# A gated block of recurrence and feed-forward layer on one core: three small groups of adding transfers, a transfer of token factors placed earlier in SyncE's list, a loop over chunks written out, and weight units of the first chunk placed earlier

## The reference

```python
def wkv(time_decay, time_first, k, v):        # along T, per channel
    w, u = -jnp.exp(time_decay), time_first
    def step(carry, kv_t):
        aa, bb, pp = carry
        kt, vt = kv_t
        q = jnp.maximum(pp, u + kt)
        e1, e2 = jnp.exp(pp - q), jnp.exp(u + kt - q)
        y_t = (e1 * aa + e2 * vt) / (e1 * bb + e2)
        q2 = jnp.maximum(pp + w, kt)
        e1b, e2b = jnp.exp(pp + w - q2), jnp.exp(kt - q2)
        return (e1b * aa + e2b * vt, e1b * bb + e2b, q2), y_t
    ...

def ffn(x, W1, W2, W3):
    hidden = jax.nn.silu(x @ W1.T) * (x @ W3.T)
    return fwht(hidden) @ W2.T

x = x + jnp.tanh(g_xattn[0]) * wkv(time_decay, time_first, layernorm(x), ctx)
x = x + jnp.tanh(g_ffn[0]) * ffn(layernorm(x), W1, W2, W3)
```

## Time and profile before

| | |
|---|---|
| three runs | median 1058.67 us (1058.36 to 1063.57) |
| profiled execution | 1061.08 us, span 1059.3 us |
| PE, DVE, ACT, POOL busy | 1002.8, 805.1, 440.5, 239.9 us |
| mean share of the 16 DMA engines in use | 0.94 from 100 to 150 us, 0.49 from 400 to 500 us |

### The profile page before, as it was taken

How to read it: one execution, slowest core, us unless ns; L and a number is a source line. 1 busy time by engine, 2 the same in 40 slices (tenths; PEclk the granted TensorE clock), 3 DMA queues, 4 the chain that set the end, 5 groups by cost and what they waited for, 6 DMA issues and landing times.

```text
span 1059.3 us, 18211 instructions
## 1 busy us (share of the span) xinstructions
PE 1002.8 (95%) x6892; PEld 684.3 (65%) x6892; DVE 805.1 (76%) x1316; ACT 440.5 (42%) x736; POOL 239.9 (23%) x180
## 2 busy tenths in 40 slices
PE   5799998769999999999999999999999999999998
PEld 2365443346677777777776677776777777767775
DVE  7857998869989995889667995889669994653334
ACT  5766451336244443455243443455243542422221
POOL 0130121101432133221421033321422124211111
PEclk9899999889999999999999999999999999999999
DMA  9977999994885446354644356354745434444331
GB/s 357 319 284 267 286 263 307 216 328 168 292 290 188 153 187 239 120 200 152 265 160 180 127 193 238 105 201 161 268 163 178 155 126 159 160 159 156 131 153 40
DMA packets 47398, 214.27 MB, mean 202 GB/s; under 512 B 9200, under 2 KB 24688, under 8 KB 36208
## 3 DMA queue, kind: packets, MB, share of 16 engines
q1 hardware_dynamic: 40816, 200.52, 51.7%
q0 software_dynamic: 6496, 12.58, 5.7%
HBM read 183.70 MB, written 41.97 MB: 213 GB/s over the span
## 4 chain that ended last, share of the span: by engine, by line
PE 66%; DVE 13%; DMA 12%; issue 6%; ACT 2%; SPq 1%; POOL 0%; DVEq 0%; ACTq 0%
PE pl L743 8%; PE pl L741 8%; PE pl L742 8%; PE po L753 7%; PE po L755 7%; PE pg L741 6%; PE pg L742 6%; PE pg L743 6%; DMA up_sums<-w_t 5%; DMA up_sums<-up_sums 4%; PE po L764 4%; PE po L762 4%; DVE x L1435 1%; DVE work L1628 1%; DVE eb L1284 1%
## 5 line engine op out<-in xcount | busy, mean ns | idle before, releaser
L1756 POOL TENSOR_TENSOR work<-work 128x512 bf16<-128x512 f32 x112 | 164.2, 1466 | 604.6 <-DVE work L1628 604.6
L753 PE MATMUL po<-work,w 128*128 128x512 f16 x456 | 173.0, 379 | 1.7 <-DVE x L1435 0.7
L755 PE MATMUL po<-work,w 128*128 128x512 f16 x456 | 172.8, 379 | 0.0
L1071 ACT ACTIVATE work<-work 128x256 f32<-128x256 f32 x168 | 68.0, 415 | 210.1 <-DVE work L1535 209.9
L741 PE MATMUL pg<-wts 128*128 128x256 f16 x448 | 122.5, 273 | 13.5 <-DVE work L1535 13.4
L1535 DVE TENSOR_TENSOR work<-pl,wts 128x256 f32<-128x256 f32 x168 | 65.2, 415 | 81.5 <-PE pl L743 79.9
L741 PE MATMUL pl<-xn,wts 128*128 128x256 f16 x448 | 122.4, 273 | 0.0
L743 PE MATMUL pg<-wts 128*128 128x256 f16 x448 | 122.4, 273 | 0.0
L742 PE MATMUL pl<-wts 128*128 128x256 bf16 x448 | 122.4, 273 | 0.0
L741 PE MATMUL pl<-wts 128*128 128x256 f16 x448 | 122.4, 273 | 0.0
L743 PE MATMUL pl<-wts 128*128 128x256 f16 x448 | 122.4, 273 | 0.0
(11 more groups left out here) (207 smaller groups left out, 2138.3 us busy)
## 6 DMA issues: line engine op xcount, KB each, us to landing
wts<-up_stage SPq DMA_DIRECT2D x56, 2048.0 KB, 7.9
up_stage<-wts SPq DMA_DIRECT2D x8, 1024.0 KB, 10.2
up_stage<-wts SPq DMA_DIRECT2D x16, 512.0 KB, 7.9
ev<-ctx_t SPq DMA_DIRECT2D x7, 1024.0 KB, 10.3
xin<-x_t SPq DMA_DIRECT2D x7, 1024.0 KB, 7.6
bv<-x_tok SPq DMA_DIRECT2D x7, 1024.0 KB, 9.6
out_t<-x SPq DMA_DIRECT2D x7, 1024.0 KB, 4.5
wts<-w_t SPq DMA_DIRECT2D x4, 1024.0 KB, 11.6
```

The costliest lines, as they stand in the source:

```text
L753: pe.matmul(po[:, d, :], w2h[:, j, d * P:d * P + P], hh[:, b, :], start=start, stop=False, skip_group_check=True)
L755: pe.matmul(po[:, d, :], w2l[:, j, d * P:d * P + P], hh[:, b, :], start=False, stop=False, skip_group_check=True)
L1071: act.activation(sg[:, slot, cols], src, ACT.Silu, scale=(1.0, -1.0)[slot]).then_inc(acted, 1)
L1756: pool.tensor_tensor(hl[:, b, :], hf[:, slot, :], hh[:, b, :], ALU.subtract).then_inc(pair_lo, 1)
```

## The change

There are five edits.

- `GROUPS` becomes three groups of two pieces each.
- In SP's list, `put_sums(6)` and `spread_factors(Run(3))` now stand ahead of `load_again(8)`, and `load_tokens(1)` ahead of `load_unit(10)`.
- The loop over runs 3 to 6 is written out (`middle_runs`), with constant counts.
- `unit_hi(4)` and `unit_lo(4)` move from slot 0 of run 1 to beside slot 3 of run 0; `unit_hi(5)` stands ahead of the work on the second weights in slot 0; units 5 to 11 move a slot or less ahead (`unit_slot`).
- The moments of run 3's tokens (`next_tok`) move from slot 12 to slot 11.

```diff
 FIRST_AT = dict(tok=2, tok_norm=3, exps=((4, 0), (4, 2), (5, 0), (5, 2)), weigh=6, scan_b=6, den=7, log=7, scan_a=7,
                 num=8, inv=8, over=9, resid=9, mean=(11, 1), centre=10, square=11,
-                sum_var=11, var=(13, 0), rsqrt=13, norm=14, next_tok=12)
+                sum_var=11, var=(13, 0), rsqrt=13, norm=14, next_tok=11)
...
-GROUPS = ((2, 4), (4, 8))
+GROUPS = ((2, 4), (4, 6), (6, 8))
...
-        def run_loop(eng, body):
-
-            with eng.Fori(0, 2) as i:
-                body(Run(i * 2 + 3, 0, i + 1))
-                body(Run(i * 2 + 4, 1, i + 1))
+        def middle_runs(body):
+
+            for r in range(3, 7):
+                body(Run(r, 1 - r % 2, (r - 1) // 2))
...
-        unit_slot = {0: (4,), 1: (5, 6), 2: (7, 8), 3: (9,), 4: (10, 11), 5: (12,), 9: (13,), 10: (14,), 11: (15,)}
+        unit_slot = {0: (5, 6), 1: (7, 8), 2: (9,), 3: (10,), 4: (11,), 5: (12,), 9: (13,), 10: (14,), 11: (15,)}
...
             load_x(1)
-            load_unit(10)
             sp.wait_ge(xn_turned, 4)
             load_tokens(1)
+            load_unit(10)
             load_unit(11)
...
             put_factors(Run(3))
+            put_sums(6)
+            spread_factors(Run(3))
             load_again(8)
-            spread_factors(Run(3))
-            put_sums(6)
             load_again(9)
...
-            run_loop(sp, steady)
+            middle_runs(steady)
...
                     if j == 0:
+                        unit_hi(5)
                         for i in range(11, 14):
                             tile_hi(i)
...
                     for n in unit_slot.get(j, ()):
-                        unit_hi(n)
+                        if n > 5:
+                            unit_hi(n)
...
             turned_hi(1)
+            unit_hi(4)
             silu(a, 3)
...
             hidden_tile(a, 3)
+            unit_lo(4)
             ffn(b)
```

More of the change, by code:

```diff
@@ L861, in _ @@
             pairs(Run(2, 1, 0))
-            run_loop(pe, pairs)
+            middle_runs(pairs)
             pairs(Run(7, 0, 3))
@@ L1166, in _ @@
             pairs(Run(2, 1, 0))
-            run_loop(act, pairs)
+            middle_runs(pairs)
             pairs(Run(7, 0, 3))
@@ L1670, in _ @@
             hidden_tile(a, 3)
+            unit_lo(4)
             ffn(b)
             pairs(Run(2, 1, 0))
-            run_loop(dve, pairs)
+            middle_runs(pairs)
             pairs(Run(7, 0, 3), more=False)
@@ L1778, in _ @@
             pairs(Run(2, 1, 0))
-            run_loop(pool, pairs)
+            middle_runs(pairs)
             pairs(Run(7, 0, 3))
```

## The result

The changed kernel takes 1056.82 us (median of 12 runs, 1054.86 to 1059.82), the kernel before beside it on the same chip 1061.01 us. The ratio is 0.9967, with an interval of 0.9953 to 0.9981: a gain of 0.33%, some 4 us, where 13.3 us were predicted. The time lies above the predicted range.

The account below looks back on a forecast made before the run. The prediction took DVE's list to bound the kernel up to about 285 us and PE's after it. Gains of 8.8 + 1.0 + 3.5 = 13.3 us from 1058.67 gave 1045.4 us, range 1039.5 to 1051.5.

Parts of the forecast that it names:

- Part 1: Weight units and run 2's tokens, slots 0 to 5: DVE takes slot 5's tile sooner, 1.5 us (bounds 0.7 and 1.7).
- Part 2: Moments in slot 11 cover slot 12's 4.18 us stop, less 0.7 us waiting for tokens: 3.5 us (bounds 2 and 4.2).
- Part 3: Spread of run 3's factors ahead of the scaling: it starts at 210.0 instead of 218.83, 8.8 us including both earlier parts.
- the factors land near 202.9: Ahead of the scaling: the factors land behind run 2's big load, no sooner than before, and the spread lands at 209.9.
- rival B: Thicker DMA crowd in 140 to 200 us; tokens, sums' buffer or factors come later: 7.0 us gained, 1051.7 us; chance 0.23.
- The ring order: Run 3's factors share a ring with run 2's 2 MB load, consumed in order, so they cannot pass it.
- the 4.2 forecast: Ahead of the scaling, 4.2 us of DVE's 8.01 us wait stay: it starts at 210.0 and not at 205.8.
- Part 4: Clock in pair 0: PE waits less, so half of DVE's 2.06 us stop goes, 1.0 us (bounds 0 and 2.1).
- The prediction's own formula: PE's wait in pair 0: 8.31 us, plus 5.0, minus the 8.8 gained up to the scaling, gives 4.5 us.
- Part 5: Loop over runs 3 to 6: without the jump back its stop goes, 3.5 us (below 3.0, or 4.1 with the loop's ends).
- C: Front edits do nothing, another transfer releases the scaling at the old time; only the loop's 3.5 us: 1055.2 us; chance 0.07.
- D: The third group of adding transfers is late and holds later loads and PE: 33 us slower, 1092 us; chance 0.03.

Follow-up runs that it names:

- e2: The changed kernel with the adding transfers in the two groups of before, all other edits kept: 1053.72 us, ratio 0.9923.
- e15: The kernel before with the three groups of adding transfers and nothing else: 1060.31 us, ratio 0.9987.
- e5: The changed kernel without the adding transfers, so the weights of units 4 to 15 are wrong: 1046.29 us, ratio 0.9844.
- e7: The changed kernel with run 3's factors written as 128 pieces instead of 1024 and read back in a wrong order: 1044.75 us, ratio 0.985.
- e10: The changed kernel, three groups, with every run's factors written in 128 pieces and read back correctly with a stride: 1065.12 us, ratio 1.0036.
- e13: The changed kernel, three groups, with the factors of run 3 alone in 128 pieces, read back with a stride: 1049.76 us, ratio 0.9877.
- e14: The changed kernel with two groups and the factors of run 3 alone in 128 pieces, read back with a stride: 1048.05 us, ratio 0.9873.
- e3: The changed kernel with run 3's factors put ahead of put_sums(5) and of run 2's first load in SP's list: 1055.71 us, ratio 0.9932.
- e4: The changed kernel with run 3's factors issued by ScalarE in slot 13 instead of by SP: one run, 1050.27 us, the kernel before 1060.90 beside it.
- e6: The changed kernel measured again, unchanged: 1055.91 us, ratio 0.9944.
- e8: The changed kernel with the third group's adding transfers held until the factors have landed: 1060.02 us, ratio 0.9979.
- e1: The kernel before with only its loop over runs 3 to 6 written out: 1059.74 us, ratio 0.9983.
- e9: The changed kernel with two groups and run 3's tokens, moments, factors and spread moved sooner: 1053.6 us, ratio 0.9936.

## Why the prediction was wrong

**Part 1 was right.** It said 1.5 us. DVE took slot 5's tile at 110.57, 37.49 us from the mark; before it was 109.57 - 70.52 = 39.05. That is 1.6 us. The stop of 3.39 us stayed, and PE's product was what DVE waited for, as put.

**Part 2 was right in its sum, 3.5 us, in part by luck.** Both parts made DVE free for the scaling 5.0 us sooner, exactly the sum. In detail it differed: the tokens were there without a wait, and a new stop of 1.61 us for the next sums' buffer stood behind them. With these edits but two groups (e2) DVE waited 1.56 us for the tokens and was free 3.6 us sooner, of which Part 2 has 2.0, its lower bound. e15 shows, besides, that the three groups alone take 2.4 us off the stop of 4.18: the edits cover the same wait, and their gains don't add.

**Part 3 failed,** at the step "the factors land near 202.9", that is, at their flight of 14 us. From the mark, the scaling began at 145.3 us where it had been 148.3: 3.0 us gained and not 8.8. The flight was taken as 14 us because "they stood behind" the big load. Without the adding transfers it is 14.5 us (e5), with 128 pieces 13 to 15 (e7, e10, e13, e14): for the floor the figure was good. On SP's queue they did run behind the load: in the changed kernel 21 and 13 packets under 512 bytes are recorded in 191 to 194 and 194 to 197 us, while that queue moved 1.21 and 1.07 MB, and 295 in the next 3 us. But that was not what made the flight long: put ahead of the load (e3), or on another queue (e4), they took 26.5 and 27.1 us. What the step left out is the turn-taking with the packets of the other queues (e4), here those of the adding transfers, which makes it 18.3 us in two groups (e2) and 22 to 23 in three (the changed kernel, e6). Without those adds (e5, and e8, where only the third group was held: 13.9 us) or with few small packets (e7) it is gone. From the mark the factors were issued 2.6 us sooner than before (115.7 against 118.3) and landed at 138.6, where 132.4 had been put. The third group's adds begin at 188.05 and 190.67 us, with the factors issued at 188.79. So the edit of the groups worked against that of the spread, inside one change; the mechanism belongs to rival B, but the working had no price for it.

I had the rows for a doubt: the earlier trace rows show 443 packets of 512 to 2048 bytes beside 560 small ones, and I read only the small ones. (They ran 8 to 14 us behind their issue, not 9 to 14.) I also took the window in which the small packets were recorded for the landing, where e5 has 6.7 us between the two.

The Trainium skill, page DMA: Bandwidth & Descriptors, section Queues, rings and completion order, says that a DMA engine takes turns between the rings it has work for, a packet at a time. The equal counts on the three queues of e4 agree, and the 368 beside 339 here; in the other two windows shown above they are 295 beside 320 and 302 beside 197. The ring order that I cited from the same section agrees with the packets on SP's queue, but it did not decide the landing.

**With two groups the prediction's steps come nearer.** From the mark, e2's scaling began at 213.27 - 72.19 = 141.1, 7.2 us sooner than before (8.8 put). Its stop of 4.35 us is near the 4.2 forecast because two terms were off alike: DVE was free 1.4 us later than put, and the factors landed 2.1 us later. In all e2 gained 9.7 us from the mark, 8.5 between the medians, of the 13.3.

**Part 4 failed with Part 3.** It said 1.0 us. PE after, in pair 0, against the earlier trace rows:

```profile
225.94 0.40 PE L740 MATMUL pg<-wts 128*128 128x256 f16 x1 [7.60 <-DVE work L1537]
```

That is 7.60 us where 4.5 were put; the clock fell as before and DVE's stop stayed at 2.06 us. The prediction's own formula would give 8.31 + 5.0 - 3.0 = 10.3 us for this wait, so it was off as well. Where the stop ahead of the scaling was halved (e2), DVE's stop was 0.98 us, as the term has it, but behind a wait of PE of 2.99 us; with 2.64 us (e4) there was no such stop, and with 1.96 us (e14) it was 1.16. Taking half of 2.06 was a guess that e2 happened to meet.

**Part 5 had the right mechanism, and a term was missing.** The stop at the jump back is gone, 3.5 us. But the other intervals are longer by 0.34 us in the mean, so 1.8 us stay (e1, and 593.58 - 591.80 here). I had seen that the runs outside the loop were 0.3 us longer and counted this as a possible gain; it was the price.

**The sum by what ran:** 3.0 ahead of the scaling, 0 for the clock, 1.8 for the loop: 4.8 us from the prediction's terms, 4.3 measured from the mark, 4.2 between the medians. Of the rivals, B is nearest in kind but gave 7.0 (its 1051.7 us lies just outside the range that was to reach over most of it). C gave 1055.2 with another mechanism (another transfer releases the scaling at the old time). D did not happen.

**Still open:** why turns cost as much as they do. 1024 packets of 4 bytes pass in 3 us without adds, and take three or four such windows beside them. In the trace of the kernel before, the adding packets take about 0.16 us each where they are alone (140 packets, 45.6% of 16 engines in 206 to 209 us), and in e3, with as many small packets beside them, 0.36 us (156 packets, 117.4% in 194 to 197). They are slow in themselves, then, and slower in company; what a packet waits for is not shown. Nor is it shown what makes a written-out run longer.

## What to carry to other kernels

When a small scattered transfer gates a step, look at what else is in flight in its window, by count of packets and not by bytes, and ask of every other edit whether it puts more there. A transfer's landing is read from what it releases, not from when its packets are recorded. Fewer pieces cure it, but if an engine then reads with a stride, the price is paid at every read: pack only the transfer that gates, and leave the steady part as it is.

## What the runs showed of the hardware

- A write of 1024 elements of 4 bytes took 14.5 us to report without adding transfers beside it, 18.3 with them in two groups (at most 15.9 when issued sooner, e9), 21.8 and 22.9 in three, and 26.5 and 27.1 in three when put ahead of the load (e3) or on ScalarE's queue (e4). 128 pieces of 32 bytes took 12.8 to 14.8 us beside the same adds.
- Three queues with work had equal numbers of packets in 3 us, whatever their size: 119, 117 and 117 (e4).
- VectorE's product or sum of 128x1024 elements takes 0.81 us more (1.61 to 2.42, and 1.21 to 2.02 us) when one f32 operand is read at a step of 32 bytes, with its access cut in two dimensions. The Trainium skill, page SBUF — State Buffer, section Door 1: The DMA port swizzle, says that reads which cross to a new line of 16 bytes each time pay a penalty; the rows agree.
- A run written out takes 118.2 to 118.6 us, one inside the loop 117.9, one that enters or leaves the loop 118.2, and the jump back cost 3.5 us once.
- The time from a fixed row early in the program repeated to 0.3 us between two executions of the changed kernel (984.5 and 984.2 us), while its 12 runs lie 5 us apart.
